# The gate keeps its scaled logits and weights in h's PSUM bank, and its pick is folded into two neighbours

## The reference, cut to what matters

```python
x = x + tanh(g_xattn) * fake_quant(layernorm(x)) @ fake_quant(ctx)      # "main"
y = layernorm(x)
logits = y @ route_w.T                       # 8 per row
topk_v, topk_idx = top_k(logits, 1)
route_weight = one_hot(topk_idx) * topk_v
h = einsum('bsd,erd->bser', y, A)            # 8 x 16 per row
wh = route_weight[..., None] * h
x = x + tanh(g_ffn) * einsum('bser,eor->bso', wh, Bw)
```

## Time and profile before

| what | us |
|---|---|
| median of 3 runs (389.13 to 390.45) | 389.33 |
| the profiled execution's own time | 389.91 |
| its span, first to last instruction | 388.1 |
| PE busy | 338.8 (87%) |
| DVE busy | 292.3 (75%) |
| ACT busy | 186.1 (48%) |
| POOL busy | 166.4 (43%) |
| mean granted TensorE clock | 0.987 |

### The profile page before, as it was taken

One profiled execution on the slowest core, in us unless ns is written; L12 is line 12 of the kernel. 1 busy time (PEld: TensorE's weight loads), 2 busy tenths in 40 slices (PEclk: granted clock), 3 DMA queues, 4 the chain that ended last, 5 costly groups with the idle time before them and its releaser, 6 DMA issues.

```text
span 388.1 us, 5794 instructions
## 1 busy us (share of the span) xinstructions
PE 338.8 (87%) x2204; PEld 186.8 (48%) x2230; DVE 292.3 (75%) x578; ACT 186.1 (48%) x119; POOL 166.4 (43%) x219
## 2 busy tenths in 40 slices
PE   0169899999999879998596999999999899998883
PEld 0145344657667536435162364645464546464461
DVE  3989975787988888875688576798764566758785
ACT  1697574868668414488289442422640602440020
POOL 2766566232113740389449226183635162524000
PEclk9999999999999999999699899999999999999999
DMA  7999999096557995999989943976849961277625
GB/s 304 407 366 386 395 387 353 22 389 207 177 194 277 185 233 199 353 246 320 190 131 331 252 150 69 315 160 192 213 85 249 230 118 20 54 119 169 258 110 216
DMA packets 93618, 87.63 MB, mean 226 GB/s; under 512 B 71812, under 2 KB 72836, under 8 KB 89476
## 3 DMA queue, kind: packets, MB, share of 16 engines
q1 hardware_dynamic: 93568, 87.11, 76.4%
q10 hardware_dynamic: 12, 0.00, 0.0%
HBM read 52.49 MB, written 16.78 MB: 178 GB/s over the span
## 4 chain that ended last, share of the span: by engine, by line
PE 64%; DVE 19%; DMA 10%; issue 3%; ACT 2%; POOL 1%; ACTq 0%; DVEq 0%
PE main L1407 44%; DMA qa<-q 6%; PE hp L1428 3%; PE hp L1432 3%; PE hp L1429 3%; PE outp L1470 3%; PE outp L1472 2%; PE outp L1471 2%; DVE whs L1007 2%; DVE pick L993 2%; DVE bn L839 2%; DMA xs<-in_x 2%; DVE xs L1015 1%; DMA prow<-in_g_ffn 1%; DVE wh L996 1%
## 5 line engine op out<-in xcount | busy, mean ns | idle before, releaser
L1407 PE MATMUL main<-q,qa 128*128 128x512 bf16 x875 | 204.7, 387 | 6.8 <-DMA qa<-q 2.4
L1407 PEld LDWEIGHTS main<-q,qa 128*128 128x128 bf16 x896 | 87.8, 99 | 110.2 <-issue 7.2
L533 POOL TENSOR_TENSOR yn<-y,yn 128x2048 f16<-128x2048 f32 x12 | 48.9, 4075 | 32.9 <-ACT y L694 32.7
L967 DVE SCALAR_TENSOR_TENSOR xs<-main,cc,xs 128x512 f32<-128x512 f32 x52 | 38.6, 743 | 29.8 <-PE main L1407 29.6
L540 POOL CAST q<-c 128x2048 bf16<-128x2048 int8 x24 | 45.2, 1905 | 24.9 <-ACT c L650 17.1
L650 ACT ACTIVATE c<-stage,zpc,inv 128x2048 int8<-128x2048 f32 x24 | 49.6, 2086 | 11.2 <-DMA stage<-in_ctx 11.1
L518 POOL TENSOR_SCALAR ve<-mv 128x1 f32<-128x1 f32 x16 | 3.5, 220 | 90.8 <-DVE mv L974 90.8
L1015 DVE SCALAR_TENSOR_TENSOR xs<-outp,tsc,xs 128x512 f32<-128x512 f32 x52 | 36.8, 734 | 6.0 <-PE outp L1472 5.8
L688 ACT ACTIVATE yn<-xs,sc 128x2048 f16<-128x2048 f32 x10 | 20.9, 2092 | 42.5 <-POOL sc L527 42.5
L662 ACT ACTIVATE x<-xs,sc 128x2048 int8<-128x2048 f32 x13 | 27.2, 2090 | 27.6 <-POOL sc L513 25.1
L839 DVE BATCH_NORM_STATS2 bn<-xs 128x6 f32<-128x512 f32 x52 | 32.0, 676 | 7.8 <-DMA xs<-in_x 7.8
(11 more groups left out here) (122 smaller groups left out, 423.6 us busy)
## 6 DMA issues: line engine op xcount, KB each, us to landing
stage<-in_ctx SPq DMA_DIRECT2D x24, 1024.0 KB, 7.6
xs<-in_x SPq DMA_DIRECT2D x13, 1024.0 KB, 6.7
out<-xs SPq DMA_DIRECT2D x12, 1024.0 KB, 5.7
yT<-in_ctx SPq DMA_DIRECT2D x4, 1024.0 KB, 10.6
y<-in_ctx SPq DMA_DIRECT2D x4, 1024.0 KB, 10.6
c<-in_x SPq DMA_DIRECT2D x3, 1024.0 KB, 7.1
out<-c SPq DMA_DIRECT2D x3, 1024.0 KB, 6.3
c<-in_L_ffn_A SPq DMA_DIRECT2D x1, 1024.0 KB, 15.9
```

Of the source, the lines that this page charges most:

```text
L533: pool.tensor_tensor(yn[:, 1, :], y[:, :], yn[:, 0, :], ALU.subtract).then_inc(s_ylo_made, 1)
L967: dve.scalar_tensor_tensor(out=xcol(t, c0, c1), in0=mainp[n % 2][:, :], scalar=cc[:, :], in1=xcol(t, c0, c1), op0=ALU.mult, op1=ALU.add).t ...
L1407: last = pe.matmul(mainp[n % 2][:, :], q1T(t)[:, k, :], q2[:, nb, k, :], start=(k == 0), stop=(k == KC - 1))
```

## The change

The gate's scaled logits hl and its weights wh move from SBUF into free columns of hp's own PSUM bank (144 to 279 and 288 to 415). `pick` is no longer made: one scalar_tensor_tensor compares the expert numbers eid with the index and multiplies by h in the same step. The greatest logit, which was a factor of pick, becomes a second scalar factor of tsc, so that wh is smaller by that factor and tsc greater. Since the gate now uses the bank of hp to its last instruction, h of the next tile waits for `s_wh_ready` (the gate's last write) and not for `s_h_read`.

```diff
-        hl = sb("hl", [P, WC], f32)
-        pick = sb("pick", [P, ER], f32)
-        wh = sb("wh", [P, ER], f32)
-        eid_i = wh[:, :].bitcast(i32)
+        eid_i = sb("eid_i", [P, ER], i32)
-        diag = pick
+        diag = sb("diag", [P, P], f32)
         hp = bank("hp")
+        hl, wh = hp[:, 144:144 + WC], hp[:, 288:288 + ER]
...
             def gate(t):
-                dve.tensor_tensor(hl[:, :], hp[:, 0:WC], wscale[:, :], ALU.mult).then_inc(s_h_read, 1)
-                dve.wait_ge(s_h_read, n)
+                dve.tensor_tensor(hl, hp[:, 0:WC], wscale[:, :], ALU.mult).then_inc(s_hl_done, 1)
+                dve.wait_ge(s_hl_done, n)
...
-                dve.tensor_scalar(pick[:, :], eid[:, :], idxf[:, :], top8[:, 0:1], ALU.is_equal, ALU.mult)\
-                   .then_inc(s_pick_done, 1)
-                dve.wait_ge(s_pick_done, n)
-                dve.tensor_tensor(wh[:, :], hl[:, 0:ER], pick[:, :], ALU.mult).then_inc(s_wh_done, 1)
+                dve.scalar_tensor_tensor(out=wh, in0=eid[:, :], scalar=idxf[:, :], in1=hl[:, 0:ER],
+                                         op0=ALU.is_equal, op1=ALU.mult).then_inc(s_wh_done, 1)
...
-                dve.tensor_scalar(tsc[:, t:t + 1], am[:, 1:2], th[:, 1:2], None, ALU.mult).then_inc(s_tsc_done, 1)
+                dve.tensor_scalar(tsc[:, t:t + 1], am[:, 1:2], th[:, 1:2], top8[:, 0:1], ALU.mult, ALU.mult)\
+                   .then_inc(s_tsc_done, 1)
...
-                dve.tensor_scalar(whs[:, 0, :], wh[:, :], am[:, 2:3], None, ALU.mult).then_inc(s_wh_high, 1)
+                dve.tensor_scalar(whs[:, 0, :], wh, am[:, 2:3], None, ALU.mult).then_inc(s_wh_high, 1)
                 dve.wait_ge(s_wh_high, n)
-                dve.scalar_tensor_tensor(out=whs[:, 1, :], in0=wh[:, :], scalar=am[:, 2:3], in1=whs[:, 0, :],
+                dve.scalar_tensor_tensor(out=whs[:, 1, :], in0=wh, scalar=am[:, 2:3], in1=whs[:, 0, :],
                                          op0=ALU.mult, op1=ALU.subtract).then_inc(s_wh_ready, 1)
...
             def main(t, nb, run):
-                if t in (0, TB):
+                if t < G or t == TB:
                     wait_piece(t // TB, nb, run)
...
             def h_rows_high(t):
-                pe.wait_ge(s_h_read, t)
+                pe.wait_ge(s_wh_ready, t)
...
             def norm_high(t):
-                if t == YD:
+                if t == YN[0]:
                     act.wait_ge(s_main_done, UNIT[G - 1, NB - 1] + 1)
-                    act.wait_ge(s_y_turned, 4 * YD)
...
             def norm_full(t):
-                if t > YD:
-                    act.wait_ge(s_ylo_made, t - YD)
+                s, count = y_turned(t - 1)
+                act.wait_ge(s, count)
```

More of the change, by code:

```diff
@@ L31 @@
 UNIT = {u: i for i, u in enumerate(RAMP + [(t, nb) for t in range(G, T) for nb in range(NB)])}
-QD = 6
-YD = 3
-YP = {0: 0, 1: 1, 2: 2, T - 1: YD}
+QT = [0, 1, 2, 3, 4, 5]
+YT = [0, 1, 2, 15]
+QN = [t for t in range(T) if t not in QT]
+YN = [t for t in range(T) if t not in YT]
+LOW_DVE = []
+OUT_ACT = []
+OUT_DVE = [t for t in range(T) if t not in OUT_ACT]
+N4 = 0
 TURNS = [("q", 0), ("q", 1), ("q", 2), ("q", 3), ("a", 0), ("b", 0), ("q", 4), ("y", 0), ("y", 1), ("y", 2), ("q",
@@ L497, in _ @@
             pool.wait_ge(s_eid_made, 1)
-            pool.tensor_copy(eid[:, :], eid_i).then_inc(s_eid_ready, 1)
+            pool.tensor_copy(eid[:, :], eid_i[:, :]).then_inc(s_eid_ready, 1)
             def first_norm(t):
@@ L545, in widen_x, with add_part @@
                 pool.wait_ge(s_q1_seen, t)
[L546 to L549, removed]
+                s, count = q1_turned(t - 1)
+                pool.wait_ge(s, count)
                 pool.tensor_copy(q1[:, :], x8[:, :]).then_inc(s_q1_ready, 1)
+            def add_part(t, g):
+                pool.wait_ge(s_part_made, NB * OUT_ACT.index(t) + g + 1)
+                pool.tensor_tensor(xcol(t, g * NW, (g + 1) * NW), xcol(t, g * NW, (g + 1) * NW), part[:, g * NW:(g + 1) * NW], ALU.add)\
+                    .then_inc(s_part_added, 1)
             first_norm(0)
@@ L715, in _, with scale_part @@
             act.wait_ge(s_zpc_ready, 1)
+            def scale_part(t, g):
+                act.wait_ge(s_out_done, NB * t + g + 1)
+                act.wait_ge(s_tsc_done, t + 1)
+                act.activation(part[:, g * NW:(g + 1) * NW], outp[g % 2][:, :], ACT.Identity, bias=zero[:, :], scale=tsc[:, t:t + 1])\
+                   .then_inc(s_part_made, 1)
             affine_x(0)
@@ L872, in widen_x @@
                 if t:
-                    dve.wait_ge(s_q1T_turned, 2 * t)
+                    s, count = q1_turned(t - 1)
+                    dve.wait_ge(s, count)
                 dve.tensor_copy(q1[:, :], x8[:, :]).then_inc(s_q1_ready, 1)
@@ L1058, in norm_group @@
                 if g == 0:
-                    dve.wait_ge(s_ylo_made, t - YD)
+                    s, count = y_turned(t - 1)
+                    dve.wait_ge(s, count)
                 dve.tensor_scalar(y[:, c0:c1], xcol(t, c0, c1), sc2[:, t, 1:2], sc2[:, t, 2:3], ALU.mult, ALU.add)\
@@ L1467, in expert_product @@
                 if NB * t + g >= 2:
-                    pe.wait_ge(s_outp_read, NB * t + g - 1)
+                    s, count = outp_emptied(t, g - 2) if g >= 2 else outp_emptied(t - 1, g + 2)
+                    pe.wait_ge(s, count)
                 o = outp[g % 2][:, :]
```

100 lines of the change are left out of this document (66 added, 34 removed).

## The result

The changed kernel takes 377.05 us, the median of 4 runs (374.85 to 377.79), beside 389.89 for the kernel before (389.13 to 390.77, 4 runs). The ratio is 0.9661 with a 95% interval of 0.9614 to 0.9708. Run once more later, beside 11 runs of the kernel before, it gave 377.45 and 0.9686 (0.9657 to 0.9714). So it is about 12.5 us faster. The forecast was 8.55 us faster (381.0). Direction and mechanism held, but the forecast gain was about 4 us too small. The median itself, 377.05, is just inside the range that ended at 376.8; carried over to the 389.33 that the forecast started from, it is 0.9661 x 389.33 = 376.1 and just outside.

What follows compares the result with a forecast made beforehand. TensorE sets the end, delayed by gate instructions that GpSimd holds. Gates 2, 3, 5, 6, 13 and 14 with 15: 0.25 + 1.0 + 0.25 + 5.4 + 1.15 + 0.5 = 8.55 us, so 381.0 us, range 376.8 to 385.2.

Steps and rivals of the forecast that it cites:

- What bounds it, and the holds: TensorE sets the end; GpSimd holds nine gate instructions in tiles 3, 5, 6 and 13; all nine holds go.
- The gate's own length: Each of 16 gates changes by -0.25 us, bounds -0.32 and +0.11; counts only at gates 2, 14 and 15.
- the guard of 0.3 us: Upper allowance in the gate's length for its two results now written to PSUM, both together.
- The new wait: h of the next tile waits for the whole gate; always met when TensorE gets there, cost 0.
- the slow clock behind the stop: Half clock on TensorE behind its new stop at h of tile 6, expected to cost 2.9 us again.
- gates 6, 13, 14 and 15: Later gates' gains: 5.4 us at 6, 1.15 at 13, 0.5 for 14 and 15 together.
- Gate 3, alone: TensorE's 2.35 us gap behind tile 3's gate goes, but transfers bind the stretch behind: gain 1.0, between 0 and 2.35.
- Gate 5, alone: Gap of 5.47 us and 2.9 of slow clock go, mostly returning at h of tile 6: net 0.25, -0.3 to 3.15.
- Gate 6: Gap of 3.69 us behind tile 6's gate and 1.7 of slow clock go: gain 5.4, at least 3.7.
- Gate 13: TensorE's gap behind tile 13's gate goes: gain 1.15 us, bounds 0.65 to 1.15.
- B: Rival, 24%: clock stays up, or transfers behind gate 3 follow fully; gain 10 to 13 us, time 376.3 to 379.

Runs made afterwards that it cites:

- The short subtraction: Kernel before, old gate kept, with GpSimd's subtraction for the low part of y cut from 2048 to 512 columns: 378.33 us, 0.9667.
- the kernel without any new gate: Changed kernel with the old SBUF gate put back for every tile, h still waiting for the whole gate: 388.93 us, 0.9992 to the kernel before.
- gate 3 alone: Changed kernel with the old SBUF gate for all tiles but 3: 386.04 us, 0.9917 to the kernel before.
- gate 5 alone: Changed kernel with the old SBUF gate for all tiles but 5: 385.5 us, 0.9888 to the kernel before.
- gate 6 alone: Changed kernel with the old SBUF gate for all tiles but 6: 385.52 us, 0.9897 to the kernel before.

## Why the prediction was wrong

**What bounds it, and the holds**: right. The nine long instructions were held by GpSimd, and no form with an operand in PSUM is held. One reading was a little off: the nine end up to 0.14 us behind GpSimd's end, not within 0.1. The short subtraction shows the cause, the kernels with one buffer moved back show the condition.

**The gate's own length**: right. It is 0.20 us shorter where 0.25 was forecast. The first half of whs costs +0.065 from PSUM (342 against 277 ns in the kernel with the weights in SBUF), where 0.07 was taken: half of 128 columns at the 1.03 ns a column of the earlier trace rows. Why it is half, no run shows. MAX8 and the reduction add 5 ns each (170 to 175, 286 to 291), and the two results written to PSUM about 9 ns each (the first product 299 to 308; the new one 347 with its result in SBUF, 356 in PSUM), far below the guard of 0.3 us. The Trainium skill's figures (VectorE: DVE Perf Modes, The TRN2 errata) would have added an estimated 0.39 us a gate; the trace shows nothing of the kind. The copy into SBUF for many operations that the Trainium skill advises there (Rules for kernel authors) is what the old gate has, and there the holds are.

**The new wait**: right, 0 (the kernel without any new gate, 0.9992).

**Where the 4 us are, in the changed kernel itself.** Up to h of tile 6 the sum had 0.25 + 1.0 + 3.15 = 4.4 us; measured are 7.19 (192.35 for 199.54). TensorE starts there as soon as the transpose has landed, at 192.22, so only that landing counts, and it came 4.2 us earlier than the 196.4 of before. The transpose was issued 1.40 earlier and took 9.4 us to land instead of 12.2. The step that failed is the one that took this landing as it had been: "landed 12.2 us later, at 196.4 ... Only 3.15 us were to spare". That is 2.8 us. The other 1.2 are the slow clock behind the stop, set at 2.9 us, measured 1.7. Together they are the 4 us: with gates 6, 13, 14 and 15 as forecast it is 7.19 - 1.7 + 5.4 + 1.15 + 0.5 = 12.5, beside 13.0 us between the profiles at turn_wh(15) and 12.1 between their spans. Why the landing took less time stays open: it took 9.3 to 9.6 us in all six profiles in which no instruction of gate 5 is held and SyncE's order is unchanged, and 10.3 to 12.2 in the others of that order.

**Gate 3, alone**: wrong by 2.5 us, 3.50 for 1.0. The step that failed is "transfers start at most 1.66 us earlier, while a transpose still occupies the engines", and from it the choice of 1.0. The bound itself was nearly right in the changed kernel: the store of tile 2 is issued 1.96 us earlier (144.14), as soon as the transpose is out of the queue. But that is not where the gain is read. The product of tile 7 started 3.06 us earlier (169.71 for 172.77; some 0.4 of it is gate 2's), because its transpose, issued 1.72 earlier, also landed in 4.8 us instead of 6.1, for which no run shows the reason. In the changed kernel only the 1.40 us by which the transpose of tile 6 was issued earlier reach h of tile 6; with gate 3 alone TensorE doesn't wait there, and the whole of it shows. I took the DMA share of 0.95 as a wall of work, when the chain through it was one of waits: store, then load, then statistics, then transpose. Of such a chain each link starts when the one before has landed, and with gate 3 alone what was taken off its front came out at its end: 3.03 us at the store, 3.14 at the issue of the transpose. The bound of 1.66 was itself a matter of the one execution it was read from: in the profile without a new gate the transpose ahead of the store was out of the queue at 142.92, not 144.44. The end of the range for this gate, 2.35, was too low too, as the gap is not an upper bound if the queue ahead of it also moves.

**Gate 5, alone**: wrong by 2.1 us, 2.35 for 0.25 by the profile, within its bounds (up to 3.15), and perhaps more by the runs (4.4). The new stop came where it was foreseen, with half clock behind it. In the changed kernel the stop was 4.14 us instead of the 5.2 forecast, and the half clock lasted 3.41 us instead of 6.83. But the shorter stop doesn't explain the shorter half clock ("nearly as long as before, and I expect the same half clock behind it"): with gate 5 alone the stop was shorter still, 3.70, and the half clock was 6.82 long and cost 2.8, much as forecast. What this profile gains is then 3.57 - 2.8 = 0.8 at tile 6 and 1.4 at gate 6, 2.2 of its 2.35. In the changed kernel the same term is 8.4 - 4.14 - 1.7 = 2.5. That the two come out nearly equal is chance.

**Gate 6**: 4.77 for 5.4 in the profile, 4.0 by the runs, inside its bounds of 3.7 to 5.4. **Gate 13**: its gap is gone; the 1.15 was not measured alone.

**Not foreseen**: the half clock in the tail, for 3.40 us. Up to turn_wh(15) the profiled execution was 13.0 us ahead (366.91 for 379.90), at the last two adds of VectorE 11.8 (371.40 for 383.19): 1.2 us.

**The sum** was 8.55; with the measured terms of gates 3, 5 and 6 it is 8.55 + 2.5 + 2.1 - 0.6 = 12.55. That it meets the 12.5 so closely is partly luck, as each of the three is uncertain by 1 us or more. Of the rivals, B (24%) was the one that came true, for reasons of its kind: the transfers were done earlier, and the slow clock was shorter. The range ended just inside B's faster edge.

## What to carry to other kernels

Before shortening a small VectorE instruction that is sometimes ten times as long as its median, look at what GpSimd does at that time; here moving one of its wide operands to PSUM freed it, and cost 5 to 65 ns. When a stop goes away, ask of each transfer behind it what it waits for: a chain of store, load and transpose can move as a whole even while the DMA engines look full, and its landing times can change too, so an old landing is no fixed point. A queue that is reordered for one transfer can delay the engines that wait for another. Where TensorE waited for 4.1 and 5.5 us here, useless matmuls in the gap paid.

## What the runs showed of the hardware

GpSimd's casts hold VectorE as its subtraction does, each until it ends (up to 1.87 and 4.16 us); a reduction from the same SBUF tile takes its 0.29 us undisturbed. How long the granted clock fell doesn't follow from the length of TensorE's wait alone. Of ten waits of 2.3 to 3.0 us nine had a slow stretch of 3.4 us and one had none (2.35 us: 1.00 in the kernel before, 0.58 in that with gate 6 alone). Of eleven of 3.3 to 4.2 us six had 3.4 us, four had 6.8 and one had none. All six of over 5 us had 6.8. In four profiles it fell for 3.4 us in the tail too, where their longest wait is 1.98 us. The slow stretch came behind no wait that was filled with matmuls. Its price depends on what follows: 1.6 us at h of tile 6, about 0.25 behind gate 3, where the next product waited for a transfer anyway.
